# The second attention's probabilities: from a second product of keys and queries to transposes of the exponentials

## The reference

```python
qkv = data @ W_qkv + b_qkv
q = qkv[:, :, :DIM].reshape(n, l, H, HD)
k = qkv[:, :, DIM:2 * DIM].reshape(n, l, H, HD)
v = qkv[:, :, 2 * DIM:].reshape(n, l, H, HD)
scores = jnp.einsum('nqhd,nkhd->nhqk', q, k)
attention = jax.nn.softmax(scores / jnp.sqrt(jnp.float32(HD)), axis=3)
out = jnp.einsum('nhql,nlhd->nqhd', attention, v).reshape(n, l, DIM)
return out @ W_out + b_out
```

## Time and profile before

| | us |
|---|---|
| median of three runs | 3015.39 |
| lowest and highest | 3015.31, 3015.74 |
| profiled execution, first to last instruction | 3025.9 |
| second attention within it (1839.7 to 2806.3) | 966.6 |

### The profile page before, as it was taken

One profiled execution on the slowest core, in us unless ns is written; L12 is line 12 of the kernel. 1 busy time (PEld: TensorE's weight loads), 2 busy tenths in 40 slices (PEclk: granted clock), 3 DMA queues, 4 the chain that ended last, 5 costly groups with the idle time before them and its releaser, 6 DMA issues. The chain is left out here.

```text
span 3025.9 us, 50008 instructions
## 1 busy us (share of the span) xinstructions
PE 2770.4 (92%) x17716; PEld 1938.1 (64%) x17716; DVE 2107.9 (70%) x4508; ACT 1731.9 (57%) x3340; POOL 1752.1 (58%) x1540
## 2 busy tenths in 40 slices
PE   7999999999999999989994787999999999999376
PEld 6995565656656565648883674666666666665276
DVE  5667777777777777666776435877877778777632
ACT  5665777776776767676772343544544545445142
POOL 0004989898898989891110573555555555555067
PEclk9999999999999999989996798999999999999588
DMA  3015444444544545420002331000000000000033
GB/s 101 1 58 129 119 117 117 115 114 109 130 106 113 123 106 131 105 71 5 23 15 67 72 60 33 2 5 5 9 5 6 5 9 5 5 6 9 28 84 50
DMA packets 146695, 179.65 MB, mean 59 GB/s; under 512 B 31571, under 2 KB 76176, under 8 KB 145936
## 3 DMA queue, kind: packets, MB, share of 16 engines
q1 hardware_dynamic: 132368, 165.72, 21.7%
q0 software_dynamic: 14080, 10.73, 2.7%
HBM read 56.51 MB, written 17.72 MB: 25 GB/s over the span
## 5 line engine op out<-in xcount | busy, mean ns | idle before, releaser
L1982 POOL TENSOR_TENSOR arena<-arena 128x512 f32<-128x512 f32 x1152 | 1447.0, 1284 | 565.7 <-ACT arena L1325 450.8
L1605 DVE TENSOR_REDUCE top<-psum 128x1 f32<-128x512 f32 x1536 | 974.6, 677 | 196.0 <-PE psum L917 123.6
L1325 ACT ACTIVATE arena<-psum 128x512 f32<-128x512 f32 x1536 | 840.8, 600 | 240.7 <-PE psum L917 141.3
L909 PE MATMUL psum<-stack 96*128 96x512 f32 (+1 forms) x2048 | 627.5, 426 | 16.5 <-ACT arena L1325 9.3
L960 PE MATMUL psum<-arena,values 128*32 128x512 f32 (+1 forms) x3072 | 477.6, 597 | 3.4 <-ACT arena L1325 3.4
L909 PEld LDWEIGHTS psum<-stack 96*128 96x128 f32 (+1 forms) x2048 | 344.0, 191 | 198.1 <-DVE top L1605 87.7
L960 PEld LDWEIGHTS psum<-arena,values 128*32 128x32 f32 (+1 forms) x3072 | 134.0, 119 | 290.0 <-issue 284.8
L917 PE MATMUL psum<-stack 64*128 64x512 f32 x2048 | 292.5, 399 | 11.8 <-DVE top L1605 5.6
L1951 POOL TENSOR_SCALAR rstd<-mv 128x4 f32<-128x4 f32 x56 | 13.0, 233 | 480.0 <-DVE mv L1466 478.1
L1636 DVE RECIPROCAL psum<-psum 128x128 f32<-128x128 f32 x256 | 228.5, 934 | 25.3 <-PE psum L999 25.3
L917 PEld LDWEIGHTS psum<-stack 64*128 64x128 f32 x2048 | 200.4, 184 | 59.0 <-issue 26.0
(11 more groups left out here) (189 smaller groups left out, 3895.3 us busy)
## 6 DMA issues: line engine op xcount, KB each, us to landing
stack<-halves SPq DMA_DIRECT2D x768, 128.0 KB, 2.3
qk_ring<-qk_split SPq DMA_DIRECT2D x64, 256.0 KB, 2.9
v_ring<-v_split SPq DMA_DIRECT2D x32, 256.0 KB, 3.0
tokens<-xn SPq DMA_DIRECT2D x16, 256.0 KB, 2.4
...
```

The source lines that it names most:

```text
L909: return T_.matmul(bk, st[0:k, side, h, cols], st[0:k, 1 - side, h, :], start=True, stop=True)
L1325: S_.activation(prob[l][tile % N_PROB[l]][:, h, :], psum[:, bank[key], :], ACT.Exp, scale=scale).then_inc(released[bank[key]], 1)
L1605: give(V_.reduce_max(top[i][:, column:column + 1], psum[:, bank[key], :], AX.X), key)
L1982: ins = G_.tensor_tensor(to[:, h, :], old[:, h, :], prob[l][tile % N_PROB[l]][:, h, :], ALU.add)
```

## The change

In the second attention the scores are computed once, with queries on the partitions. VectorE stores the negative maxima in `peak`, and the bank stays held. ScalarE reads the same bank, takes the exponential with the row's maximum as bias (an operand in memory) into `by_query`, and puts the row's sum into `row_sum` by the instruction's sum output (`exps`). VectorE inverts two sums at a time (`shares`), and GpSimd multiplies each row of `by_query`, 128 by 512, by its share, in place. TensorE turns the scaled rows (`turns`): each 128x512 tile in eight transposes of 64 queries by 128 keys, in two 64-row tiles of the array, each half into a bank of its own. ScalarE copies the bank of the lower half, VectorE that of the upper one, into `by_key`, from where `weigh` takes them. Its result is final and goes straight to `mixed`. The second product with its DMAs, `total`, the product with ones, the reciprocals on 128x128 pieces and the last multiplication are gone from this attention. The scale 1/8 moves into the q weights and biases (once, `SHARP`).

`Ring.give` now moves the bank to the ring's end, so `take` hands out the bank that was released longest ago. This holds for all rings; in the second attention "o" moves from `products` to `other`. The rows lie in the arena (four) and in `stack2` (eight), twelve in all, so an exponential waits for the turn of the row twelve before it. The second line of `WHEN` has new numbers; the first one's are the same. Buffer declarations and unchanged waits are left out of the diff.

```diff
-    dict(rows=(1.82, 1.82), queries=(0.75, 0.75), keys=(0.80, 0.80), values=(1.01, 1.01), maxima=(1.04, 1.48),
-         probs=(3.03, 3.47), last=(3.43, 4.05), sums=(4.38, 4.38), mix=(4.38, 4.83), out=(4.93, 4.97),
-         ahead=(-1.52, 0.45), route=(5.03, 10.53), ranks=(9.80, 10.86), keep=(10.00, 10.00)))
...
+    dict(queries=(0.615, 0.660), keys=(0.605, 0.605), values=(1.177, 1.210), maxima=(1.000, 1.750),
+         exps=(1.048, 1.808), shares=(1.340, 2.257), turns=(1.896, 2.647), last=(2.753, 2.877), out=(3.443, 3.443),
+         ahead=(-1.963, 0.391), route=(5.882, 10.521), ranks=(9.538, 10.463), keep=(10.404, 10.404)))
...
-            queue("last", (l, n), 2, 2, n)
+            queue("last", (l, n), (2, 5)[l], (2, 5)[l], n)
...
             else:
-                queue("probs", (l, n), heads * TILES_B, heads * TILES_B, n)
-                queue("sums", (l, n), 1, 1, n)
-            queue("mix", (l, n), 5, 5, n)
+                queue("exps", (n,), heads * TILES_B, heads * TILES_B, n)
+                queue("shares", (n,), TILES_B, TILES_B, n)
+                queue("turns", (n,), heads * TILES_B, heads * TILES_B, n)
...
 
     def give(self, key):
         self.busy.remove(self.at[key])
+        self.places.remove(self.at[key])
+        self.places.append(self.at[key])
...
     def maxima(self, l, n):
-        at_once = HEADS[l] if l else 1
-        for i in range(0, HEADS[l] * TILES_B, at_once):
-            for j in range(i, i + at_once):
-                self.once(self.products, ("score", l, n, j))
-            for _ in range(at_once):
-                yield
+        for i in range(HEADS[l] * TILES_B):
+            if l == 0:
+                self.once(self.products, ("score", l, n, i))
+            elif i % HEADS[l] == 0:
+                for j in range(i, i + HEADS[l]):
+                    self.products.take(("score", l, n, j))
+            yield
+
+    def exps(self, n):
+        for j in range(HEADS[1] * TILES_B):
+            self.products.give(("score", 1, n, j))
+            yield
+
+    def turns(self, n):
+        for j in range(HEADS[1] * TILES_B):
+            if j % HEADS[1] == 0:
+                for h in range(HEADS[1]):
+                    self.once(self.products, ("turn", n, j + h))
+            yield
 
     def rows(self, l, n):
-        self.once(self.products if l else self.other, ("top", l, n))
+        self.once(self.other, ("top", l, n))
         yield
...
     def probabilities(self, l, n):
         for kt in range(TILES_B):
...
     def last(self, l, n):
-        ring = self.products if l else self.mixed
+        ring = self.other if l else self.mixed
         if l:
             ring.take(("o", l, n))
-        yield
+        for _ in range(4 if l else 1):
+            yield
         ring.give(("o", l, n))
...
+            def turns(n):
+                for j in range(HEADS[1] * TILES_B):
+                    if j % HEADS[1] == 0:
+                        at = n * HEADS[1] * TILES_B + j
+                        pe.wait_ge(scaled, at + HEADS[1])
+                        banks = [place(("turn", n, j + half)) for half in range(2)]
+                        for i in range(TILES_B * HEADS[1]):
+                            kt, h = divmod(i, HEADS[1])
+                            for half, (bk, done) in enumerate(banks):
+                                part, cols = slice(half * HALF, (half + 1) * HALF), slice(kt * P, (kt + 1) * P)
+                                ins = T_.matmul(bk[:, i * HALF:(i + 1) * HALF], by_query[(at + h) % N_ROWS][part, cols],
+                                                ident[part, part], is_transpose=True, tile_position=(half * HALF, 0))
+                                if i == TILES_B * HEADS[1] - 1:
+                                    ins.then_inc(done, 1)
+                    yield
+
...
                 width = WIDTH[l]
...
+                    for h in range(HEADS[l]):
+                        pe.wait_ge(*read(("turn", n, HEADS[l] * (TILES_B - 1) + h)))
+                else:
+                    pe.wait_ge(*read(("prob", l, n, kt, HEADS[l] - 1)))
                 pe.wait_ge(*read(("v", l, n | 1)))
                 if kt == 0 and free(("o", l, n)):
...
                 for h in range(HEADS[l]):
                     c = slice(width * h, width * (h + 1))
                     ins = T_.matmul(bk[c, :], values[:, n % N_VALUES, kt, c],
-                                    prob[l][(n * TILES_B + kt) % N_PROB[l]][:, h, :],
+                                    by_key[n % 2][:, kt, h, :] if l else prob[(n * TILES_B + kt) % N_PROB][:, h, :],
                                     start=kt == 0, stop=kt == TILES_B - 1, tile_position=(0, width * h))
...
                 for kt in range(TILES_B):
                     cols = slice(kt * P, (kt + 1) * P)
                     for h in range(HEADS[l]):
-                        if l == 0:
-                            bk, done = place(("prob", l, n, kt, h))
-                            product(bk, st, 1, h, cols, 98).then_inc(done, 1)
-                        elif h == 0:
-                            both_heads([("prob", l, n, kt, head) for head in range(HEADS[l])],
-                                       [(hv[:, k, cols], hv[:, q, :]) for q, k in ((QH, KH), (QL, KH), (QH, KL))]
-                                       + [(ones_rows[n % N_STACK], top_rows[n % N_STACK])])
+                        bk, done = place(("prob", l, n, kt, h))
+                        product(bk, st, 1, h, cols, 98).then_inc(done, 1)
                         yield
-                    if kt == 2 and l == 0:
+                    if kt == 2:
                         weigh(l, n, 0)
...
 
+            def exps(n):
+                for j in range(HEADS[1] * TILES_B):
+                    i, key = n * HEADS[1] * TILES_B + j, ("score", 1, n, j)
+                    qt, h = divmod(j, HEADS[1])
+                    if i >= N_ROWS:
+                        for event in rows_turned(i - N_ROWS):
+                            act.wait_ge(*event)
+                    else:
+                        act.wait_ge(*arena_free(1))
+                    act.wait_ge(peaked, i + 1)
+                    S_.activation(by_query[i % N_ROWS], psum[:, bank[key], :], ACT.Exp, bias=peak[n % 2][:, qt, h:h + 1],
+                                  accum_out=row_sum[n % 2][:, qt, h:h + 1]).then_inc(released[bank[key]], 1)
...
+                    if j % 2 == 0:
+                        key = ("turn", n, j)
+                        act.wait_ge(*written(key))
+                        S_.activation(by_key[n % 2][:, :, :, j * HALF:(j + 1) * HALF],
+                                      psum[:, bank[key], :].rearrange("p (t h q) -> p t h q", t=TILES_B, h=HEADS[1]),
+                                      ACT.Copy).then_inc(released[bank[key]], 1)
+                    yield
+
             def last_tiles(l, n):
...
                 act.wait_ge(*tile_weighed(l, n, TILES_B - 1))
                 bk = bank["o", l, n]
-                S_.activation(weighted[l][n % 2], psum[:, bk, :], ACT.Copy).then_inc(released[bk], 1)
+                S_.activation(mixed[1][:, g, :] if l else weighted[n % 2], psum[:, bk, :], ACT.Copy).then_inc(released[bk], 1)
...
             def maxima(l, n):
                 i = n % 2
...
                 for j in range(HEADS[l] * TILES_B):
                     key = ("score", l, n, j)
-                    column = j % HEADS[l] * TILES_B + j // HEADS[l] if l else j
                     dve.wait_ge(*written(key))
-                    give(V_.reduce_max(top[i][:, column:column + 1], psum[:, bank[key], :], AX.X), key)
+                    if l:
+                        qt, h = divmod(j, HEADS[l])
+                        V_.reduce_max(peak[i][:, qt, h:h + 1], psum[:, bank[key], :], AX.X, negate=True).then_inc(peaked, 1)
+                    else:
+                        give(V_.reduce_max(top[i][:, j:j + 1], psum[:, bank[key], :], AX.X), key)
+                    yield
+
+            def shares(n):
+                for qt in range(TILES_B):
+                    dve.wait_ge(*read(("score", 1, n, HEADS[1] * qt + HEADS[1] - 1)))
...
+                    yield
+
+            def turns(n):
+                if n >= 2:
+                    dve.wait_ge(*tile_weighed(1, n - 2, TILES_B - 1))
...
+                        give(V_.tensor_copy(by_key[n % 2][:, :, :, j * HALF:(j + 1) * HALF],
+                                            psum[:, bank[key], :].rearrange("p (t h q) -> p t h q", t=TILES_B, h=HEADS[1])),
+                             key)
                     yield
 
             def rows_of_maxima(l, n):
                 i, n_top, key = n % 2, HEADS[l] * TILES_B, ("top", l, n)
                 if n >= 2:
-                    dve.wait_ge(*all_max_rows(l, n - 2))
+                    dve.wait_ge(*all_max_rows(n - 2))
...
+            def shares(n):
+                for qt in range(TILES_B):
+                    at = n * TILES_B + qt
+                    pool.wait_ge(inverted_sums, at + 1)
```

(4 more changed lines are left out.)

253 lines of the change are left out of this document (127 added, 126 removed).

## The result

| | before | changed |
|---|---|---|
| median, us | 3015.43 | 2968.03 |
| lowest and highest | 3015.31, 3015.74 | 2966.84, 2972.41 |
| ratio, 95% interval | | 0.984 (0.983 to 0.985) |
| profiled execution | 3025.9 | 2967.0 |

What follows compares the result with a forecast made beforehand. TensorE was taken to bound the kernel before, ScalarE's bank walk afterwards: 8 x 12.8 + 10.0 = 112.4 us a batch against 120.9, 68 saved over eight, 3025.9 to 2958 profiled, 2947 forecast; likeliest case 2915 to 2980.

Steps and rivals of the forecast that it cites:

- The walk through the banks: Second attention: ScalarE's chain through the PSUM banks sets 12.8 us a group; as likeliest case 12.3 to 13.3, chance 0.50.
- The opening: Start of a group's walk: first turns 0.56, scores 0.7, landing 0.26, maximum 0.65, together 2.2 us.
- ScalarE's chain: After the first maximum, ScalarE works without a gap: five exponentials at 0.75, four copies at 0.5, 5.75 us.
- TensorE's own sum: TensorE's work per group of the second attention: 10.8 us, 11.2 with four changes of tile shape at 0.1 each.
- Rival B: TensorE stays the bound and everything else hides: 11.2 us a group, 2839 us in all; chance 0.12.
- GpSimd's product: Eight row scalings a group, at most 1.28 us each, at least half: 5 to 10.3 us, hidden under 1.6 each.
- GpSimd over 1.6: GpSimd's scaling of one row takes over 1.6 us, making the kernel slower; chance 0.02.
- The exponential: ScalarE's exponential with bias from memory and sum output: 0.75 us each, range 0.58 to 0.95.
- Filling and draining: Start and end of the second attention, taken as equal before and after the change.
- The base: Profiled execution before lay 10.5 us above the median, so the forecast of 2958 became 2947 us.
- rival D: TensorE's clock falls from short idle pieces: 14.5 us a group if once in each, 3056 us; chance 0.16.
- Rivals C and E: C: exponential costs 0.95 us, 3011 in all, chance 0.15. E: 64 transposes take turns, 7.2 us a group, 3160, 0.05.

Runs made afterwards that it cites:

- no_sum: Changed kernel with exponentials giving no row sum and ones written for the inverted sums; 2969.8 us, kernel before on the same chip 3027.3.
- seven_tt: Changed kernel with seven banks instead of six, weighing's result in that ring, and GpSimd's product taking two tensors; 2906.7 us, before on the same chip 3017.3.
- pool_small: Changed kernel with GpSimd scaling only the first 64 of 512 columns of each row; 2963.3 us, kernel before on the same chip 3027.3.
- pool_tt: Changed kernel with GpSimd's product taking the share as a second tensor; 2968.1 us (before, same chip, 3027.3), repeated beside the changed kernel 2958.9 (before 3016.7).

## Why the prediction was right, and where it was wrong

**The mechanism was right in the main.** The walk through the banks sets the group, ScalarE's exponentials and copies are what TensorE waits for, and a seventh bank in the ring, with GpSimd relieved, removes it (12.09 us a group). Forecast 12.8 us a group, measured 13.03 to 13.05. The parts were less exact than the sum. The opening was forecast at 2.2 and took 2.28. I then let ScalarE's chain run "without a gap" to k's projection, 5.75 us with five exponentials. It ends for TensorE at the copy at 2219.89, after three exponentials (3.88 us), and it has a gap: ScalarE waits 0.19 us for VectorE's maximum of scores that TensorE could start only after the first exponential. From there TensorE has work for 6.73 us, which I had as 0.75 + 3.53 and 0.6 for handovers. The last turn, the last pair of scores and q's projection were missing there. One part was 1.9 us too long and the other 2.0 too short; that they cancel is luck, and the 12.8 is worth less than it looks. The wrong number of exponentials is why no_sum gave 0.28 and not 0.5 to 1.0.

**TensorE's own sum** was forecast at 10.8 to 11.2 and is 12.0 (13.03 less 1.01 of waits; 11.9 in seven_tt). Turned pairs were right: 2.47 us for 32, 0.077 a pair, forecast 0.07. Weighing 3.59 was right too. Mis-sized was the change between tile shapes: three rounds of scores cost 0.77 to 0.96 to the next instruction where I had 0.68, 3.4 for four pairs instead of 2.7, and the projections 2.6 instead of 2.3. That is 0.9 us more than their rounds, where "0.1 for each of four changes" allowed 0.4. Rival B, which was given 0.12, would have given not 2839 us but, as seven_tt shows, about 2907.

**GpSimd's product** is the term that left its bounds. I bounded it above by the sum with two inputs, 1.28, since "nothing shown is slower per element". It takes 1.57, and the same product with two tensors as inputs 1.04. The row was nearest in shape and not in form: one operation with two tensors says nothing about one with a column of scalars. The chance for "GpSimd over 1.6" was 0.02, and it missed that point by 0.03 us; it should have been weighed as a limit level with the walk. The Trainium skill (GPSIMD Engine Reference, 3.1) gives 769 ns for 512 elements as the best case of a loop. The form used here takes 1569 ns, so that figure is no price for it; by it GpSimd would have been busy for an estimated 6.2 us, half of the group.

**The others.** VectorE was forecast at 10.2 us a group and is at 10.20. The exponential was to take 0.75 us from its start to that of the next instruction; it takes 0.68, since its own 0.69 and the 0.20 behind it overlap each other and the next. Turned rows, forecast 0.5 to 0.6, last 0.59 on ScalarE, 0.48 to the next start (2217.28 to 2217.76), and 0.68 on VectorE. So ScalarE's 11.2 is 10.3. For the output projection, norms and router I had 10.0 us a batch; with GpSimd relieved it is 112.3 - 8 x 13.05 = 7.9, with its late products 8.6 to 8.9, and 10.2 in the two batches in which the clock fell. So a batch is 113.0 to 114.6 where 112.4 was forecast: the gain is 7.3 us a middle batch, not 8.5. **Over eight batches this is 10 us of the miss.**

**Filling and draining** I had "as equal", and that is another 10 us. TensorE's timeline of both kernels, the starts of the last two output projections, first before, then the changed kernel:

```profile
2702.29 1.95 PE L1027 MATMUL psum<-wout,arena 128*128 128x128 f32 x16
...
2798.87 1.38 PE L1027 MATMUL psum<-wout,arena 128*128 128x128 f32 x10
```
```profile
2641.29 1.94 PE L1065 MATMUL psum<-wout,arena 128*128 128x128 f32 x15
...
2747.14 2.05 PE L1065 MATMUL psum<-wout,arena 128*128 128x128 f32 x16
```

The last batch took 96.6 us before, 24 less than a middle one, since TensorE was the bound and its work for further groups fell away: the last two groups took 8.6 and 8.3 us. In the changed kernel it is 105.9, only 8 less, and the last two groups take 11.7 and 12.2. That gives back 9.3 us. Most of it is GpSimd's: in the last group TensorE waits twice for scaled rows, 2.35 and 2.37 us, and its clock is at 0.50 (1.2 GHz) from 2738.4 to 2745.2, so that the weighing lasts 5.22 us instead of 3.65. In pool_small that group takes 7.7 us and the last batch 99.1; the 11.7 of the group before it stays. At the start (first scores to first output projection, 137.4 and 123.6 us) 13.8 are gained; six batches in the middle give 43.7. Together 13.8 + 43.7 - 9.3 = 48.2, against 47.4 between the medians and 68 in the forecast.

**The base** took no part in the miss, though the two profiles, 59 us apart, seem to say so. I moved the forecast of 2958 for the profiled execution down by the 10.5 us by which that of before lay above the median. But that distance isn't the kernel's. The profiled execution of before started the scores of the second attention at 1839.8, that of the changed kernel at 1836.2, and had 227.1 us from the start of the last output projection to the end, against 219.8, with the same instructions: 3.5 and 7.2 us, 10.7 in all. The changed kernel's profile lies 1 us below its median. Difference against difference, 68 forecast and 47 to 49 measured, is the fair comparison.

**The clock (rival D)** hardly came. The typical group has 1.00, with 64 transposes and three short pauses in it. From 1841 us to the end of the second attention four stretches fell to 0.50 (1.2 GHz): 6.8 us at the start, 3.4 us in each of two middle batches, and the 6.8 us of the last group. The first two of them (windows; the second row's edges take in a little at 1.00), and TensorE's timeline around the second:

```profile
1847.50:1854.30 6.80, 5.73 (x50) 4.78 (x50) 3.51 (x9) 4.11 (x10) 6.80 (x5) 0.50 0.00 0
...
2120.60:2124.00 3.40, 3.40 (x15) 2.27 (x12) 1.45 (x3) 1.56 (x4) 3.40 (x3) 0.51 0.02 5
```
```profile
2117.66 0.96 PE L940 MATMUL psum<-halves 64*128 64x512 f32 x6 [0.19 <-ACT values L1321]
...
2119.97 0.72 PE L984 MATMUL psum<-cst,arena 64*128 64x64 f32 x16 [1.35 <-POOL arena L2074]
2120.50 1.59 PE L940 MATMUL psum<-halves 64*128 64x512 f32 x6
```

In the middle the fall came right behind the wait of 1.35 us for a scaled row; scores then last 1.59 us instead of 0.96, and the group takes 15.26 us where its like in the next batches, with the same wait and no fall, take 13.7. So a late engine can cost TensorE the wait and then the clock; what decides whether the fall comes, no run shows. With the fast product (pool_tt, pool_tt_beside) no stretch fell in the middle batches; with seven banks and the slow product, where TensorE waits up to 2.5 us, one fell in each of them. By the Trainium skill's rule (TensorE: Matmul & The Clock Gate, Part 4: PE-mode transpose), transposes don't count as activity for the clock in the way matmuls do. Between them stand matmuls for most of each group, and in the typical groups, with these around them, no fall came: the rule isn't refuted, but it doesn't decide here. Rivals C and E fell with the prices above: an exponential at 0.68 us, not 0.95, and 64 transposes in 2.47 us, not 7.2.
